# The turned Q and K of the next sequence copied ahead of a table load: one reordering on two engines

## The reference, cut to what matters

```python
h = layernorm(x, ln_g, ln_b)
q, k, v = (h @ Wq), (h @ Wk), (h @ Wv)            # 16 heads of 64
q = l2norm(q) * q_scale;  k = l2norm(k) * k_scale
attn = softmax(where(causal, q @ k.T * 10, -1e9))
out = (attn @ v) @ Wo;  h = layernorm(out)
gate = softmax(h @ gate_w + gate_b)               # 8 experts, all of them computed
moe = sum_e gate_e * (gelu(h @ w1_e + b1_e) @ w2_e + b2_e)
y = layernorm(moe)
```

## Time and profile before

| | us |
|---|---|
| median of 3 runs | 1340.16 (1338.81 to 1340.35) |
| profiled execution, own time | 1340.11 |
| its span, first to last instruction | 1338.4 |
| PE busy | 1180.9 (88%) |
| DVE busy | 1048.9 (78%) |
| ACT busy | 752.7 (56%) |
| POOL busy | 368.5 (28%) |

### The profile page before, as it was taken

The page is one execution under the profiler, slowest core; times in us unless marked ns, Lnnn a source line. Parts: engine busy times, 40 slices in busy tenths (PEclk is TensorE's granted clock), DMA queues, the critical chain, the costliest instruction groups (busy, mean ns, idle before and its releaser), DMA issues.

```text
span 1338.4 us, 27838 instructions
## 1 busy us (share of the span) xinstructions
PE 1180.9 (88%) x10435; PEld 954.6 (71%) x10435; DVE 1048.9 (78%) x2718; ACT 752.7 (56%) x1740; POOL 368.5 (28%) x403
## 2 busy tenths in 40 slices
PE   3584989899998989989898998989899898989978
PEld 1363768586786868778685877868587786868877
DVE  7779677888878888887888888788888778787652
ACT  4263655556565565656556465655646565564644
POOL 1151422405133150513315051331505133150100
PEclk9595989899998989989898998989999998999889
DMA  6001000000000000000000000000000000000000
GB/s 177 5 1 40 2 1 13 1 9 5 9 5 2 13 1 10 5 9 6 1 13 1 10 5 9 6 1 10 5 9 6 8 7 5 2 9 2 5 5 5
DMA packets 18724, 14.62 MB, mean 11 GB/s; under 512 B 2408, under 2 KB 16160, under 8 KB 18592
## 3 DMA queue, kind: packets, MB, share of 16 engines
q1 hardware_dynamic: 17680, 12.76, 3.3%
q10 hardware_dynamic: 912, 0.09, 0.0%
HBM read 10.75 MB, written 2.10 MB: 10 GB/s over the span
## 4 chain that ended last, share of the span: by engine, by line
PE 76%; DVE 10%; ACT 9%; issue 3%; POOL 0%; SPq 0%; DMA 0%; DVEq 0%; POOLq 0%; ACTq 0%
PE O L499 17%; PE O L415 11%; PE S L398 7%; PE U L431 4%; PE U L483 4%; PE U L484 4%; PE U L485 4%; PE J L344 4%; PE S L362 3%; PE J L309 3%; PE J L311 3%; PE J L310 3%; PE S L358 3%; PE O L422 2%; ACT hid L701 2%
## 5 line engine op out<-in xcount | busy, mean ns | idle before, releaser
L701 ACT ACTIVATE hid<-U,b1c 128x256 f32<-128x256 f32 x512 | 202.9, 474 | 202.1 <-PE U L485 201.2
L830 POOL TENSOR_SCALAR_AFFINE_SELECT P<-P 128x512 f32<-128x512 f32 x128 | 83.8, 655 | 774.3 <-ACT P L674 774.3
L499 PE MATMUL O<-w2s,hid 128*128 128x128 f32 x2048 | 251.5, 276 | 0.0
L499 PEld LDWEIGHTS O<-w2s,hid 128*128 128x128 f32 x2048 | 238.5, 192 | 2.9
L415 PE MATMUL O<-Vx,P 128*128 128x66 f32 x1536 | 200.8, 281 | 9.1 <-ACT OT L680 9.0
L1113 DVE TENSOR_TENSOR_SCAN st<-aexp,u 128x256 f32<-128x256 f32 x256 | 196.9, 769 | 4.7 <-ACT aexp L686 4.7
L415 PEld LDWEIGHTS O<-Vx,P 128*128 128x128 f32 x1536 | 183.0, 193 | 24.1 <-issue 12.5
L822 POOL TENSOR_TENSOR raw<-raw,nr 128x512 f32<-128x512 f32 x128 | 140.2, 1119 | 115.9 <-DVE nr L986 88.8
L483 PE MATMUL U<-h2h,w1h 128*128 128x256 f16 x512 | 149.3, 292 | 0.0
L484 PE MATMUL U<-h2l,w1h 128*128 128x256 f16 x512 | 148.8, 291 | 0.0
L485 PE MATMUL U<-h2h,w1l 128*128 128x256 f16 x512 | 148.0, 289 | 0.0
(11 more groups left out here) (163 smaller groups left out, 2148.6 us busy)
## 6 DMA issues: line engine op xcount, KB each, us to landing
xin<-in_L_attn_x SPq DMA_DIRECT2D x16, 128.0 KB, 2.2
xres<-in_L_attn_x SPq DMA_DIRECT2D x16, 128.0 KB, 2.4
hid<-in_L_ffn_w SPq DMA_DIRECT2D x2, 1024.0 KB, 6.2
out_dram<-fin SPq DMA_DIRECT2D x16, 128.0 KB, 1.8
raw<-in_L_ffn_Wq SPq DMA_DIRECT2D x1, 512.0 KB, 4.3
raw<-in_L_ffn_Wk SPq DMA_DIRECT2D x1, 512.0 KB, 6.6
raw<-in_L_ffn_Wv SPq DMA_DIRECT2D x1, 512.0 KB, 7.5
wos<-in_L_ffn_Wo SPq DMA_DIRECT2D x1, 512.0 KB, 11.0
```

Of the source, the lines that this page charges most:

```text
L499: last = mm(O[e % 2][:, t * P:(t + 1) * P], hid[:, e % 2, m, t * P:(t + 1) * P], w2s[:, e * FC + m, :], start=(m == 0), stop=(m == FC - 1))
L701: fn(hid[:, e % 2, f % FC, :], U[q % 2][:, m * SEQ:(m + 1) * SEQ], ACT.Gelu_apprx_tanh, bias=b1c[:, f:f + 1], scale=1.0 / WS).then_inc(gel ...
```

## The change

On ACT, `high` 0 and 1 of the next sequence move from the second loop (behind the table load and the gelus of expert 0) to just behind `copy_v` 3, ahead of `norm_qk` of the second half. On DVE, `low` 0 and 1 move from behind `add_state` 7 to just behind `scan` 7, ahead of the Newton steps of the second half. And DVE's three Newton steps of the first half move from k = 6 to k = 7. PE's, POOL's and SP's queues are unchanged, and no instruction is added or removed.

```diff
@@ ACT, body, between the loops and in the second
                 if new:
                     copy_v(i + 1, 3)
+                    high(i + 1, 0)
+                    high(i + 1, 1)
                     norm_qk(i + 1, 1)
                 with_gelu_and_tanh()
                 for m in range(NE + 2):
...
                     if old and m == 0:
                         gelus(i - 1, m)
-                    if new and m in TURN_AT:
+                    if new and m > 0 and m in TURN_AT:
                         high(i + 1, TURN_AT[m])
                         high(i + 1, TURN_AT[m] + 1)
@@ DVE, body, first loop
                     if new and k == 5:
                         norm_step(i + 1, 0, 0)
-                    if new and k == 6:
+                    if new and k == 7:
                         norm_step(i + 1, 0, 1)
                         norm_step(i + 1, 0, 2)
                         norm_step(i + 1, 0, 3)
@@ DVE, body, second loop
                         scan(i, m + 7)
                         if new and m == 0:
+                            low(i + 1, 0)
+                            low(i + 1, 1)
                             norm_step(i + 1, 1, 1)
                             norm_step(i + 1, 1, 2)
                             norm_step(i + 1, 1, 3)
                         add_state(i, m + 7)
-                    if new and m in TURN_AT:
+                    if new and m > 0 and m in TURN_AT:
                         low(i + 1, TURN_AT[m])
                         low(i + 1, TURN_AT[m] + 1)
```

## The result

The changed kernel takes 1356.4 us (median of 4 runs, 1353.9 to 1357.8), against 1339.5 us before: a ratio of 1.0132, interval 1.0113 to 1.0151. It is slower by 17 us. The forecast was 1320.5 us, range 1303 to 1335: the sign is wrong. The profiled execution took 1357.53 us, with a span of 1355.8.

The account below looks back on a forecast made before the run. PE's work was taken as the bound, its idle time and low clock as winnable. Fourteen bodies at 0.5 + 1.6 - 0.85 (17.5 us), body 0's 0.6 and 1.5 for low stretches: 19.6 off 1340.11 gives 1320.5 us, range 1303 to 1335.

Parts of the forecast that it names:

- Part one: High and low 0 and 1 earlier: PE's wait at the turn of n = 2 shrinks; 1.6 us gained a body.
- part two: Newton steps at k = 7: h2T starts earlier, PE's 0.38 us wait goes; 0.5 us gained a body.
- part three: Low clock behind the new gateT wait slows gated_b2 and expert_down 0: 0.85 us lost a body.
- the first low stretch: Low clock behind the 0.38 us wait for h2T should sometimes vanish or shorten: 0.1 us gained a body.
- Rival (c): Slower: the low stretch behind the new gateT wait is double; 1.3 us lost a body, 1358 us; chance 0.07.
- Rival (a): Clock stays up behind the new gateT wait: 2.3 us kept a body, 1307 us; chance 0.27.
- Rival (d): high 0 does not come forward, as ACT waits for the turn; 1336 us by part two alone; chance 0.04.

Follow-up runs that it names:

- The memset run: The changed kernel with POOL's one square beside the Newton steps at k = 7 replaced by a memset of the same buffer: 1335.6 us, ratio 0.9979.
- the kernel filled at L468: The changed kernel with 16 extra matmuls, results never read, on PE in front of gated_b2: 1329.4 us, ratio 0.9926.
- the two filled runs: The changed kernel with unread extra matmuls on PE: 16 before gated_b2 (L468), 1329.4 us; or 8 before gate_logits (L453), 1334.4 us.
- halves and `gateT` early: The kernel before with only high and low 0 and 1 moved, and DVE's copy gateT put in front of scan 8: 1285.3 us, ratio 0.9603.
- `gateT` early: The kernel before with DVE's copy gateT moved in front of scan 8 and nothing else: 1339.9 us, ratio 1.0005.

## Why the prediction was wrong

Part one, the halves, was right in its mechanism and sizes. PE's wait in front of the turn of n = 2 went from 3.87 to 1.50 us (forecast 1.5), L468 came at 9.57 us (9.75), the new wait for `gateT` is 2.07 us (2.4), and the queues behind the moved copies went as said: the table load came at 734.95, 3.75 us behind `expert_up` 0 against 1.56 before, 2.2 us later as worked out, and `expert_up` 1 did not lose by it. By itself this part gave 12 us, against (1.6 - 0.85) x 14 = 10.5 in the sum.

The step that failed is the one in part two, by which `h2T` starts at 635.4 instead of 636.12 and PE's 0.38 us wait for it goes. It priced the steps by POOL's order at k = 6, where they had stood, and not at k = 7, where they went. In the earlier trace rows `nu` took 0.77 us beside a square, POOL's timeline of before:

```profile
632.40 1.04 POOL L814 TENSOR_TENSOR sq<-raw 128x512 f32<-128x512 f32 x1
```

The same price had to be paid by the steps at their new place, where a mask and a square stand, and I counted them at the price of a resting POOL. DVE did win a lead of 0.97 us at the `divide` in front of them (719.17 against 720.14, which is the 634.98 of before shifted by 85.16 so that `weigh` in front of L453 starts at the same time in both bodies). DVE's timelines of before and after:

```profile
634.98 0.17 DVE L1018 RECIPROCAL rr<-O 128x4 f32<-128x4 f32 x1
```

```profile
719.17 0.17 DVE L1020 RECIPROCAL rr<-O 128x4 f32<-128x4 f32 x1
```

Then the steps, now behind that point, took 1.66 us, and `h2T` started at 721.97 against 721.28: 0.7 us later than before, not 0.7 earlier. The wait was 1.06 us instead of none. The memset run shows the cause: without the square's reads it is 0.27. The term stood at +0.5 us a body in the sum, and the column "rest" lost 0.70: 1.2 us, or 17 in fourteen bodies.

The second term that was mis-sized is part three, the clock. I took half a low stretch behind the new wait, 0.85 us; in the full change it was a whole one in every body: L468 to `expert_up` 2 went from 3.14 to 4.67 us, 1.53, or 10 us more in fourteen bodies. And I took it that the first low stretch would shorten, by 0.1 us a body. With the longer wait for `h2T` it became 10.2 us long in six of them, 0.63 us a body on the mean, 10 us off. 17 + 10 + 10 = 37 us covers the distance of 36 from 1320.5 to 1356.4.

Rival (c) named a double low stretch as the way to a slower kernel, and gave 1358. The time is near, the place is not: the long stretches stand behind the wait for `h2T` (L453), and behind `gateT` they are single. Rival (a), the clock stays up behind the new wait, has its time in no run, but the kernel filled at L468 shows its mechanism, worth 22 us there. Rival (d) is 1 to 3 us off by its own terms: part two alone, 0.38 to 0.5 us a body, gives 1333 to 1335, not 1336; nothing hangs on it. The TensorE: Matmul & The Clock Gate page of the Trainium skill, section HAM oscillation, warns of long idle gaps; here no idle time of PE in the fourteen bodies was longer than 2.1 us, shorter than the 3.87 of before, and the low stretches cost more. In every body of the full change the clock fell behind waits of 1.06 and 0.56 us. But such waits do not always do it: in the kernel filled at L468 the wait at L453 is as long, and in six of the fourteen bodies no low stretch follows.

What is shown, and what is not: that PE's idle time in front of L453 and L468 makes the clock fall, and what each costs, is shown by the two filled runs. Which bodies get the long stretch is not explained here: 6 of 14 in the full change, 3 with the Newton steps alone, none with the halves alone, 3 in the kernel filled at L468, 3 with the halves and `gateT` early, one before. These counts are of one execution of each kernel. The times of one kernel go with its granted clock (halves and `gateT` early: 1290.8 us at 0.947, 1281.7 at 0.954), so they may differ from one execution to the next, and a difference of one body says nothing.

## What to carry to other kernels

A step moved to another place in a queue meets other neighbours, on its own engine and on the one whose reads hold it up, here POOL: read that engine's timeline at the new place before pricing the step. Once a wait is removed, the value is set by what is late next, and it can be one copy in the wrong place of a queue: the halves gave 1%, `gateT` early nothing, the two together 4%. And cost the waits of PE with the clock they bring: here 1.5 us of slow matmuls came behind a 2 us wait, and useless matmuls in that wait made the kernel 27 us faster.

## What was unexpected of the hardware

Two edits that gave 0.9904 and 1.0070 by themselves gave 1.0132 together, 21 us more than their product, and eight useless matmuls a body took 22 us of that away. Bodies 8 and 9 of the full change have the same waits (1.06, 0.56, 0.97 and 2.07 us among them), and yet the first is 78.8 us long and the second 81.6: the low stretch behind L453 is 3.4 us in the one and 10.2 in the other.

Beside a GpSimd memset of 128 x 512, a VectorE operation of 128 x 32 with two SBUF inputs took 0.19 us, as without POOL; beside a square of the same buffer it took 0.98 us, and another beside the mask 0.51. Each held-up one ended 0.04 to 0.06 us behind POOL's instruction (721.03 behind 720.99, 722.05 behind 721.99), so its price was what was left of that instruction when it came. `nu`, which began 0.02 us behind the start of the mask, was not held up.
